# Layer-norm sums of squares moved from VectorE to ScalarE, and one transpose moved behind a projection, in a two-stage linear-attention kernel

## What is computed

```python
x = x + 0.5 * (layernorm(x) @ sign(weight).T)                    # FFN 1
Q, K, V = (layernorm(x) @ W.T + b for each of q, k, v)           # 16 heads of 64
Q, K = elu(Q) + 1, elu(K) + 1
KV = einsum('bhnd,bhne->bhde', K, V);  Z = K.sum(axis=2)
o  = einsum('bhnd,bhde->bhne', Q, KV) / (einsum('bhnd,bhd->bhn', Q, Z) + 1e-6)
x = x + o @ Wo.T + bo
x = x + 0.5 * (layernorm(x) @ sign(weight).T)                    # FFN 2
```

## Time and profile before

| | us |
|---|---|
| time, median of 2 runs (2219.35 to 2221.76) | 2220.55 |
| the profiled execution's own time | 2219.56 |
| its span on its slowest core (core 1), first to last instruction | 2218.0 |
| spans of the 8 cores | 2206.6 to 2218.0 |
| TensorE, VectorE, ScalarE busy | 1837.7, 921.8, 1091.1 |

### The profile page before, as it was taken

One profiled execution on the slowest core, in us unless ns is written; L12 is line 12 of the kernel. 1 busy time (PEld: TensorE's weight loads), 2 busy tenths in 40 slices (PEclk: granted clock), 3 DMA queues, 4 the chain that ended last, 5 costly groups with the idle time before them and its releaser, 6 DMA issues.

```text
span 2218.0 us, 33065 instructions; the slowest of 8 cores (2206.6 to 2218.0 us)
## 1 busy us (share of the span) xinstructions
PE 1837.7 (83%) x10784; PEld 807.0 (36%) x10784; DVE 921.8 (42%) x2305; ACT 1091.1 (49%) x1769; POOL 147.5 (7%) x274
## 2 busy tenths in 40 slices
PE   0588888988888888888898888878888888888887
PEld 0233333333333333333333333334444444444443
DVE  2243343434343434343433334324555555555554
ACT  1455556565656565655566565643333333333333
POOL 1000000000000000000000000000000000000000
PEclk9999999999999999999999999989999999999999
DMA  8522222222222213121222222112333333333332
GB/s 177 111 83 62 82 63 82 73 71 74 70 84 62 82 62 111 62 82 62 81 64 81 63 81 79 47 65 95 119 119 119 119 116 115 118 119 119 119 112 90
DMA packets 134630, 199.34 MB, mean 90 GB/s; under 512 B 88384, under 2 KB 88384, under 8 KB 134464
## 3 DMA queue, kind: packets, MB, share of 16 engines
q0 software_dynamic: 32960, 109.08, 14.9%
q1 hardware_dynamic: 101504, 88.15, 13.0%
HBM read 104.87 MB, written 83.89 MB: 85 GB/s over the span
## 4 chain that ended last, share of the span: by engine, by line
PE 42%; DVE 25%; ACT 16%; issue 13%; DMA 3%; DVEq 1%; ACTq 1%; SPq 0%
PE pA L463 22%; PE pA L474 14%; DVE y2t L348 4%; DVE u1b L351 3%; DVE u2b L288 3%; DVE y1t L285 3%; DVE red1b L294 3%; ACT u2b L448 3%; DVE y2t L295 3%; ACT mnb L400 3%; ACT mxb L402 3%; PE pA L478 2%; ACT nb L367 2%; PE pA L468 2%; PE tpB L453 2%
## 5 line engine op out<-in xcount | busy, mean ns | idle before, releaser
L474 PE MATMUL pA<-wv,u1fm 128*128 128x512 bf16 x1024 | 310.6, 459 | 157.2 <-ACT kbK L404 157.2
L463 PE MATMUL pA<-sw,u2fm 128*128 128x512 bf16 x1024 | 234.6, 383 | 76.7 <-DVE y2t L348 75.9
L365 ACT ACTIVATE lnb<-vr 128x1 f32<-128x1 f32 x192 | 37.9, 197 | 523.4 <-DVE vr L245 523.1
L474 PE MATMUL pA<-wk,u1fm 128*128 128x512 bf16 x1024 | 242.4, 379 | 18.5 <-ACT kbQ L388 18.5
L388 ACT CAST kbQ<-pA 128x512 bf16<-128x512 f32 x64 | 37.5, 585 | 421.3 <-PE pA L468 421.3
L463 PE MATMUL pA<-wo,attnfm 128*128 128x512 bf16 x1024 | 235.2, 383 | 2.0 <-DVE y3t L328 1.1
L463 PE MATMUL pA<-sw,u0fm 128*128 128x512 bf16 x1024 | 235.1, 383 | 0.0
L463 PE MATMUL pA<-wq,u1fm 128*128 128x512 bf16 x1024 | 232.1, 380 | 0.0
L474 PEld LDWEIGHTS pA<-wv,u1fm 128*128 128x128 bf16 x1024 | 104.6, 111 | 317.6 <-issue 258.2
L285 DVE SCALAR_TENSOR_TENSOR y1t<-pA,xt 128x1024 f32<-128x1024 f32 x63 | 77.2, 1225 | 267.6 <-PE pA L463 267.6
L319 DVE TENSOR_TENSOR phiQ<-eb,mxb 128x1024 bf16<-128x1024 bf16 x64 | 44.3, 693 | 313.8 <-ACT mxb L402 313.8
(11 more groups left out here) (120 smaller groups left out, 2449.4 us busy)
## 6 DMA issues: line engine op xcount, KB each, us to landing
xt<-x SPq DMA_DIRECT2D x64, 512.0 KB, 3.8
y1scr<-y1t POOLq DMA_DIRECT2D x64, 512.0 KB, 3.8
y1in<-y1scr POOLq DMA_DIRECT2D x64, 512.0 KB, 4.4
out<-y3t SPq DMA_DIRECT2D x64, 512.0 KB, 2.7
qscr<-qfm POOLq DMA_DIRECT2D x64, 256.0 KB, 3.1
qfin<-qscr POOLq DMA_DIRECT2D x64, 256.0 KB, 4.6
qfm<-phiQ SPq DMA_TRANSPOSE x512, 2.3
stg<-wfT SPq DMA_DIRECT2D x4, 512.0 KB, 8.5
```

Source lines behind the costliest of these rows:

```text
L463: mm = e.matmul(dst[:, h*512:(h+1)*512], lhs_fm[:, c*P:(c+1)*P], w_sb[:, c, h*512:(h+1)*512], start=(c == 0), stop=(last and c == 7))
L474: mm = e.matmul(dst[:, h*512:(h+1)*512], lhs_fm[:, c*P:(c+1)*P], w_sb[:, c, h*512:(h+1)*512], start=(c == 0), stop=(last and c == 7))
```

## The change

The squares of the second and third norm move from VectorE (`scalar_tensor_tensor`, y times y with an accumulator) to ScalarE (`activation` with `Square` and an accumulator). The scratch tiles and the sums `sq2b` and `sq3b` stay the same. Two semaphores that were declared but not used, `sSq2` and `sSq3`, tell VectorE that the sum is there. In stage B, TensorE's output projection and its transposes of `u2b` change places. The squares of the first norm (line 295) stay on VectorE.

```diff
@@ VectorE, stage A, before the loop and in iteration t
-            v.wait_ge(vY1, 1)
-            vsync(v, v.scalar_tensor_tensor(u2b[:, 0, :], y1t[:, 0, :], 0.0, y1t[:, 0, :],
-                                   ALU.bypass, ALU.mult, accum_out=sq2b[:, :]))
+            v.wait_ge(sSq2, 1)
...
-                    v.wait_ge(vY1, t + 2)
-                    vsync(v, v.scalar_tensor_tensor(u2b[:, 0, :], y1t[:, (t + 1) % 2, :], 0.0,
-                                           y1t[:, (t + 1) % 2, :],
-                                           ALU.bypass, ALU.mult, accum_out=sq2b[:, :]))
...
                 if t + 1 < NT:
+                    v.wait_ge(sSq2, t + 2)
                     if t >= 2:
                         v.wait_ge(sR02, t)
@@ VectorE, stage B
-                    v.wait_ge(vY2, t)
-                    vsync(v, v.scalar_tensor_tensor(u1b[:, 0, :], y2t[:, tw % 2, :], 0.0,
-                                           y2t[:, tw % 2, :],
-                                           ALU.bypass, ALU.mult, accum_out=sq3b[:, :]))
+                    v.wait_ge(sSq3, t)
@@ ScalarE, stage A (and the same for tile 0 before the loop)
             for t in range(NT):
+                if t + 1 < NT:
+                    e.wait_ge(vY1, t + 2)
+                    e.activation(u2b[:, 0, :], y1t[:, (t + 1) % 2, :], AF.Square,
+                                 accum_out=sq2b[:, :]).then_inc(sSq2, 1)
                 e.wait_ge(tQ, t + 1)
@@ ScalarE, stage B
                     tw = t - 1
+                    e.wait_ge(vY2, t)
+                    e.activation(u1b[:, 0, :], y2t[:, tw % 2, :], AF.Square,
+                                 accum_out=sq3b[:, :]).then_inc(sSq3, 1)
                     e.wait_ge(vVr3, t)
@@ TensorE, stage B
+                if 1 <= t <= NT:
+                    if t >= 3:
+                        e.wait_ge(vY3, t - 2)
+                    proj(e, attnfm[:, (t - 1) % 2, :], wo, pA2[:, :], bor, tWo,
+                         cw=(sAttnfm, 2 * t - 1))
                 if 2 <= t <= NT + 1:
                     e.wait_ge(sU2, t - 1)
                     if t >= 3:
                         e.wait_ge(sU2fm, 2 * t - 4)
                     transposes8(e, u2b[:, (t - 2) % 2, :], tpB, tU2T)
-                if 1 <= t <= NT:
-                    if t >= 3:
-                        e.wait_ge(vY3, t - 2)
-                    proj(e, attnfm[:, (t - 1) % 2, :], wo, pA2[:, :], bor, tWo,
-                         cw=(sAttnfm, 2 * t - 1))
```

More of the change, by code:

```diff
@@ L381, in _ @@
                              scale=r01[:, :], bias=nb1[:, :]).then_inc(sU0, 1)
+            e.wait_ge(vY1, 1)
+            e.activation(u2b[:, 0, :], y1t[:, 0, :], AF.Square,
+                         accum_out=sq2b[:, :]).then_inc(sSq2, 1)
             e.wait_ge(vVr2, 1)
```

## The result

The changed kernel takes **2132.62 us** (median of 11 runs) against 2220.75 before (10 runs): ratio 0.9605, 95% interval 0.9588 to 0.9622. It is faster, as forecast, but by 88 us and not by 123, and 7.6 us above the upper end of the range. (Some executions of any of these kernels have the cores of one die at a lower clock; they are left out of every ratio, and where they pull a median, the undisturbed time is given instead.)

What follows compares the result with a forecast made beforehand. The prediction took one chain across TensorE, VectorE and ScalarE as the bound, with stage A's variance late. From 2219.56 us it took 122 for stage A and 1 for stage B, 2096.6, plus 1.0 for the median: 2097.5; range about 2084 to 2125.

Steps and rivals of the forecast that it cites:

- the late variance, paid twice: Stage A: V projection's wait costs idle time, 58 us, and the low clock behind it, 75 us.
- Stage A's step becomes that of rows 5: Stage A: iterations become like late ones without the variance delay: 19.62 us each, gap before V 1.51 us.
- Square costs 1.04 + 0.1 and is hidden: Stage A, ScalarE: pass 1.04 us plus accumulator read 0.1, covered by 3 us before kbQ, costing nothing.
- Stage B unchanged, slack 0.11: Stage B: ring stays 11.14 us per step, the attnfm copy has 0.11 us of slack; 1 us gained.
- I take 5 falls, 8 us: Stage A: TensorE's clock still falls behind the V gap 5 times, costing 8 us on the slowest core.
- The 16 cases: Two end-of-stage-A V waits on 8 cores; one showed slow matmuls, 2.85 us, the others 1.67 to 1.89.
- the high end: Whole kernel: about 2125 us, from 15 falls in stage A and 12 us of stage B's bound.
- the clock still falls: Rival, stage A: clock falls as often as before, only 58 us idle time saved, 2163 us; chance 0.12.

Runs made afterwards that it cites:

- e10_after_again: The changed kernel once more, unchanged, on a third chip; 2084.27 us, ratio 0.9400.
- e1_a_only: Against the changed kernel, stage B restored as before, so only stage A's squares are on ScalarE; 2136.45 us, ratio 0.9617.
- e5_no_exchange: Against the changed kernel, stage B's transposes of u2b stay ahead of the output projection; 2133.2 us, ratio 0.9618.

## Why the prediction was right and wrong

- *What bounds the kernel: the late variance, paid twice.* Right, and shown: filling the gap of the kernel before gave back 75.7 us (forecast 75), the shorter wait 57 more (forecast 58).
- *Stage A's step becomes that of rows 5.* Right: 19.62 to 19.64 us, Ln 0.74 behind `kbQ`, gap 1.51 to 1.53.
- *Square costs 1.04 + 0.1 and is hidden.* Size 1.06 + 0.19, hidden; one table load as before.
- *Stage B unchanged, slack 0.11.* Right in its links: statistics 1.48 us behind `y2t`'s end (forecast 1.31 to 1.80), step 11.14 to 11.15. Its gain was mis-sized, 4 us and not 1, and the traces point to the exchange for it.
- ***I take 5 falls, 8 us.*** This is the step that failed. Core 3 had 31, worth some 50 us. The 16 cases were read as independent draws, "one in sixteen would be 4 of 60, a share of one in four 15", and both the value and the high end were built on that. But two iterations at the end of a stage cannot show a repetition. In the steady stage a fall lengthens the step by 1.6 us, and on a late core the falls come back every second iteration (core 3), on two more in stretches (20 and 18 falls), on the others hardly ever. The share differs from core to core, from near 0 to one half, and since the metric is the slowest of eight cores, one such core is enough. The prediction also took the fall in the earlier trace rows as one behind a gap of 1.51 us. The row says 1.74, with one of the eight matmuls not recorded; less its 0.22 us the gap is 1.52, and behind that gap falls do come (12 of 46 in the trace after, none of 233 at 1.51). So the row said that the gap is at an edge, which is worth two cases, not a mean of them: about 2085 us and about 2130. The changed kernel took 2083.39 to 2085.14 us or 2128.91 and more; the forecast of 2097.5 was a time that no run of it gave.
- *The rival "the clock still falls"* at 2163 had the mechanism, with the share of the kernel before (43 to 48 of 62) in place of the 31 of 62 seen.

Without the falls the sum stands: 2097.5 less 8 less 3 more from stage B is 2086.5, against 2084.27 on the chip where no core was late. That 2084.27 lies inside the forecast's range is no merit of the 5 falls: there the slowest core had 2.

## What to carry to other kernels

A wait of TensorE has two prices, its length and the clock behind it; read them apart, from the duration of the first matmuls after the gap, and test them apart by filling the gap with idle matmuls. Where a change leaves a gap at a length at which the trace shows both outcomes, forecast two times, not one between them, and take the worse core. A quarter of a microsecond of matmul in such a gap was worth some 46 us (2133.2 and 2084.68 on one chip, less about 2 for stage B, whose exchange the first lacks), and needed work placed there was worth more still.

## What the runs showed of the hardware that was not expected

- The falls change steeply with the median gap: at 1.31 us (behind one matmul) one fall on eight cores, at 1.51 at most 2 of 62 per core in both traces of the changed kernel, at 1.53 up to 31, at 1.61 24 to 26 on every core. But single longer gaps can pass: in `e10_after_again` 6 of the 12 gaps of 1.79 us with all eight matmuls recorded had no fall behind them.
- A longer gap can have fewer falls: 31 at 1.53 us, 24 to 26 at 1.61. The step is longer as well; why the rhythm changes was not tried.
- The same program took 2132.62 us in one comparison and 2084.27 in another, 2.3% apart; in `e1_a_only` and `e5_no_exchange` the same core was late in every execution.
- On a late core the gap before V is 0.01 to 0.02 us longer than on the others of its chip, also in kernels in which its clock does not fall.
- An accumulator read on ScalarE is an instruction of its own, 0.19 to 0.20 us, where VectorE's takes 0.08.
